# Constant scalars read from columns, a four-step split, and tokens routed quarter by quarter with their slots fetched by indirect transfers

## The reference, cut to what matters

```python
xn = layernorm(x)
s  = attn0(xn)               # 16 heads of 8, softmax over all 512 tokens of the row, out projection
g  = silu(ffn0(xn))          # each token goes to the expert of its largest logit, 1 of 8:
                             # gelu(xn @ W1[e]) @ W2[e], 128 -> 512 -> 128
x  = x + s * g
xn = layernorm(x)
s  = attn1(xn)               # 16 heads in windows of 32, and 8 heads over 64 pooled latents, gated
g  = silu(ffn1(xn))          # two layers: shift, qkv, l2norm, rotary, local attention, gated feed-forward
out = x + s * g
```

## Time and profile before

| | before |
|---|---|
| median of the runs | 3473.93 us (3471.63 to 3474.02, 3 runs) |
| the profiled execution | 3440.83 us, its span 3439.0 us, mean granted TensorE clock 0.974 |
| TensorE busy | 3112.3 us, 90% of the span |
| VectorE busy | 2466.9 us, 72% |
| ScalarE busy | 2338.7 us, 68% |
| GpSimd busy | 1261.4 us, 37% |

### The profile page before, as it was taken

The page is one execution under the profiler, slowest core; times in us unless marked ns, Lnnn a source line. Parts: engine busy times, 40 slices in busy tenths (PEclk is TensorE's granted clock), DMA queues, the critical chain, the costliest instruction groups (busy, mean ns, idle before and its releaser), DMA issues.

```text
span 3439.0 us, 83502 instructions
## 1 busy us (share of the span) xinstructions
PE 3112.3 (90%) x34007; PEld 1889.5 (55%) x34008; DVE 2466.9 (72%) x5000; ACT 2338.7 (68%) x4758; POOL 1261.4 (37%) x799
## 2 busy tenths in 40 slices
PE   5589799999999999999999999999999999999976
PEld 5168445556564646555565656565555656464644
DVE  6432487868687877878676868778786868687643
ACT  1265467777777786777767776867777777778744
POOL 1622034333333443444333333444443333344343
PEclk9889899999999999999999999999999999999987
DMA  6256110101011111101011111111010101111000
...
DMA packets 130458, 138.95 MB, mean 40 GB/s; under 512 B 17972, under 2 KB 112542, under 8 KB 129566
## 3 DMA queue, kind: packets, MB, share of 16 engines
...
## 4 chain that ended last, share of the span: by engine, by line
PE 46%; DVE 21%; ACT 9%; POOL 6%; issue 4%; DMA 2%; SPq 2%; POOLq 0%; ACTq 0%; DVEq 0%
PE bank L1882 5%; PE bank L1319 4%; DVE turn_f L2056 4%; PE bank L698 4%; PE bank L1926 3%; ACT prob_a L1388 3%; PE bank L1303 3%; PE bank L1332 3%; DVE nmax_a L1443 3%; PE bank L1868 3%; PE bank L1858 2%; PE bank L1849 2%; DVE ss L2049 2%; DVE nmax_f L2063 2%; POOL turn_f L1797 2%
## 5 line engine op out<-in xcount | busy, mean ns | idle before, releaser
L1388 ACT ACTIVATE prob_a<-bank 128x512 f32<-128x512 f32 x1024 | 564.4, 607 | 190.0 <-PE bank L1332 185.2
L1443 DVE TENSOR_REDUCE nmax_a<-bank 128x1 f32<-128x512 f32 x768 | 502.5, 684 | 161.6 <-PE bank L1303 160.5
L1791 POOL TENSOR_TENSOR rn<-ss,minus_half 128x16 f32<-128x16 f32 x128 | 377.8, 2952 | 270.6 <-DVE ss L2051 268.6
L1814 POOL TENSOR_TENSOR rs_f<-rs_f,minus_half 128x4 f32<-128x4 f32 x32 | 32.6, 1018 | 1108.2 <-DVE rs_f L1181 1108.2
L1797 POOL TENSOR_TENSOR turn_f<-turn_f 128x512 f32<-128x512 f32 x256 | 324.3, 1287 | 207.7 <-DVE turn_f L2056 207.7
L1332 PE MATMUL bank<-Qst_a,Kst_a 74*128 74x512 bf16 x1024 | 378.9, 389 | 18.9 <-ACT prob_a L1388 9.5
L1944 ACT ACTIVATE area<-bank 128x512 f32<-128x512 f32 x640 | 349.9, 603 | 63.2 <-PE bank L1882 55.2
L2056 DVE TENSOR_TENSOR turn_f<-area,rotf 128x1024 f32<-128x1024 f32 x256 | 307.6, 1219 | 8.7 <-POOL area L1801 6.2
L1303 PE MATMUL bank<-Kst_a,Qst_a 72*128 72x512 bf16 x768 | 302.2, 394 | 5.4 <-DMA Kst_a<-dk_a 1.2
L1319 PE MATMUL bank<-prob_a,V_a 128*9 128x512 f32 x2048 | 274.5, 609 | 13.2 <-ACT prob_a L1388 11.8
L1801 POOL TENSOR_TENSOR area<-turn_f,rn 128x1024 f32<-128x1024 f32 x128 | 267.5, 2090 | 19.0 <-POOL turn_f L1797 0.9
...
## 6 DMA issues: line engine op xcount, KB each, us to landing
...
```

The lines of the kernel that those rows point to most:

```text
L1388: nc.scalar.activation(dst, bk.full(act, product)[0:rows, :], func, **kw).then_inc(a_emptied["act"], 1)
L1443: nc.vector.tensor_reduce(out=nmax_a[:, g, t, j:j + 1], in_=bk.full(dve, f)[:], op=ALU.max, axis=AX.X, negate=True).then_inc(emptied, 1)
L1791: nc.gpsimd.tensor_tensor(rn[:, t % 2], ss[:, t % 2], minus_half[:], ALU.pow).then_inc(f_root, 1)
```

## The change

In the steady rows:
- `split` has four steps: the last subtraction writes the third bf16 part itself.
- The two copies of `split_max` become multiplications by a column of ones, `one_c`; the constants 1.0 of the gates and 1e-24 of the clip are read from columns too (`one_c`, `tiny_c`).
- The 0.5 of both gates is multiplied once into weights (`wo0_s`, `bo0`, `w_out_s`), and the last instruction of each gate becomes a plain addition.
- The 1/8 of the pooling goes into the two steps that follow it (`blocks_l` and the copies to `V_l`).

In the opening:
- VectorE chooses experts by quarters of 16 tiles (`choose`, eight instructions of 128 columns; a key of 8 minus the expert's number replaces the seven steps). TensorE ranks a quarter by expert and then by token with 23 matmuls (`ranks`), which makes each token's row within its quarter; three instructions (`rows_of`) bring it out.
- `xs_d` has 8192 rows, sorted within each quarter. GpSimd scatters a quarter's tiles from then on (`sort`), split around the last inverse root and the first weight loads. There is no zero fill.
- After the last quarter VectorE works out counts and bases, then a table of the row of `xs_d` for each of 39 x 256 slots (`m_slots`), then `pos`.
- Slots are fetched by GpSimd with two indirect gathers per block (`slots`) and no longer by SP. It issues them up to four blocks ahead, after the transposes of the block that had the ring's place (`m_slotT`).
- The first quarter is normalised right after its statistics, and GpSimd takes the first three inverse roots ahead of the head's. The early small loads are ten where they were seven; new are three tables (`expert_key`, `quarter_row`, `slot_at`).

All tables of order (`OPEN`, `TIMES`, `SEATS`) are new, and `STEP` is 179.028 where it was 177.917. In the new order 71 of row 0's 153 attention elements stand ahead of the first block's transposes, and the other 82 between the transposes and matmuls of the first blocks, the bulk ahead of block 13.

```diff
+        one_c, tiny_c = sb("one_c", [P, 1]), sb("tiny_c", [P, 1])
+        blocks_l = sb("blocks_l", [NL, LH])
...
-        xs_d = nc.dram_tensor("xs_d", [SLOTS, E], F32, kind="Internal").ap()
+        xs_d = nc.dram_tensor("xs_d", [B * T, E], F32, kind="Internal").ap()
...
             yield 5
             sp.wait_ge(s_zeroed, 1)
-            zeros, rows = turn_f[:].rearrange("p r t -> p (r t)"), xs_d.rearrange("(p r) f -> p (r f)", p=P)
-            fills = range(0, SLOTS * E // P, 4 * T)
-            for at in fills:
-                n = min(4 * T, SLOTS * E // P - at)
-                sp.dma_start(rows[:, at:at + n], zeros[:, 0:n]).then_inc(m_filled, 16)
...
-                if j + XS < NBLK:
-                    sp.dma_start(slot_ring[:, (j + XS) % XS], slot_rows(xs_d, j + XS)).then_inc(m_xs[j % XS], 16)
...
+            def inverse_root(c):
                 pool.wait_ge(m_var, c + 1)
                 nc.gpsimd.tensor_tensor(m_rs[:, c % 2, 1, :], m_rs[:, c % 2, 0, :], m_half[:], ALU.pow).then_inc(m_rstd, 1)
+
+            def sort(tiles):
+                for n in tiles:
+                    nc.gpsimd.indirect_dma_start(
+                        out=xs_d, out_offset=bass.IndirectOffsetOnAxis(ap=m_row[:, n:n + 1], axis=0),
+                        in_=x_tile(n), in_offset=None).then_inc(m_sorted, 16)
+
             def weights(j):
                 nc.gpsimd.indirect_dma_start(
                     out=w_ring[j % WS], out_offset=None, in_=W12,
                     in_offset=bass.IndirectOffsetOnAxis(ap=m_offs[:, j:j + 1], axis=0)).then_inc(m_w[j % WS], 16)
 
-            yield 82
-            pool.wait_ge(m_filled, 16 * len(range(0, SLOTS * E // P, 4 * T)))
-            pool.wait_ge(m_pos, 2)
-            for j in range(WS_EARLY):
-                weights(j)
-            for n in range(TILES):
-                nc.gpsimd.indirect_dma_start(
-                    out=xs_d, out_offset=bass.IndirectOffsetOnAxis(ap=pos[:, n:n + 1], axis=0),
-                    in_=x_tile(n), in_offset=None).then_inc(m_sorted, 16)
-            for j in range(WS_EARLY, NBLK):
-                yield block_slot(j - WS_EARLY) - 3
-                if j == WS_EARLY:
+            def slots(j):
+                for c in range(ST):
+                    nc.gpsimd.indirect_dma_start(
+                        out=slot_ring[:, j % XS, c], out_offset=None, in_=xs_d,
+                        in_offset=bass.IndirectOffsetOnAxis(ap=m_slots[:, j, c:c + 1], axis=0)).then_inc(m_xs[j % XS], 16)
+
+            for c in range(3):
+                yield 15 + 7 * c
+                inverse_root(c)
+            yield 38
+            pool.wait_ge(m_pos, 1)
+            sort(range(0, 6))
+            yield 46
+            inverse_root(3)
+            sort(range(6, 16))
+            for c in range(1, 4):
+                yield 50 + 12 * c
+                pool.wait_ge(m_pos, c + 1)
+                sort(range(16 * c, 16 * c + 8))
+                if c == 3:
+                    yield 91
+                    pool.wait_ge(m_pos, 5)
+                    for j in range(WS_EARLY):
+                        weights(j)
+                yield 56 + 12 * c
+                sort(range(16 * c + 8, 16 * c + 16))
+            for j in range(NBLK):
+                yield block_slot(j - XS) - 1
+                if j == 0:
+                    pool.wait_ge(m_pos, 6)
                     pool.wait_ge(m_sorted, 16 * TILES)
-                if j >= WS:
-                    pool.wait_ge(m_y, j - WS + 1)
-                weights(j)
+                if j >= XS:
+                    pool.wait_ge(m_slotT, j - XS + 1)
+                slots(j)
+                if j >= WS_EARLY:
+                    yield block_slot(j - XS) + 1
+                    if j >= WS:
+                        pool.wait_ge(m_y, j - WS + 1)
+                    weights(j)
             yield block_slot(NBLK) + 9
...
+            def ranks(c):
+
+                pe.wait_ge(m_hot, c + 1)
+                ps, first = rank_bank(c), 16 * c
+                nc.tensor.matmul(ps, tri[:], hot_bf[:, first:first + 16, :], start=True, stop=False, skip_group_check=True)
+                for m in range(15):
+                    last = nc.tensor.matmul(ps[:, NX * (m + 1):].rearrange("p (n e) -> p n e", e=NX), ones_sq[:],
+                                            hot_bf[:, first + m:first + m + 1, :].to_broadcast([P, 15 - m, NX]),
+                                            start=False, stop=False, skip_group_check=True)
+                for e in range(NX - 1):
+                    last = nc.tensor.matmul(ps.rearrange("p (n e) -> p n e", e=NX)[:, :, e + 1:], ones_sq[:],
+                                            m_held[:, c, e:e + 1].unsqueeze(1).to_broadcast([P, 16, NX - 1 - e]),
+                                            start=False, stop=(e == NX - 2), skip_group_check=True)
+                last.then_inc(m_ranks, 1)
...
+                if r % 4 == 1 and r > 4:
+                    yield 22 + 2.5 * r
+                    ranks(r // 4 - 1)
             row_logits(B - 1)
             yield 67.5
-            pe.wait_ge(m_hot, 1)
+            ranks(3)
...
+            def choose(c):
+
+                dve.wait_ge(m_logits, 4 * c + 4)
+                n = slice(16 * c, 16 * c + 16)
+                bias, key = (row.unsqueeze(1).to_broadcast(tiles_e) for row in (bg_s[:], expert_key))
+                top = m_max[:, n].unsqueeze(2).to_broadcast(tiles_e)
+                link(nc.vector.tensor_tensor(logit[:, n], by_expert(logit_bank(c)), bias, ALU.add))
+                link(nc.vector.tensor_reduce(out=m_max[:, n], in_=logit[:, n], op=ALU.max, axis=AX.X))
+                link(nc.vector.tensor_tensor(first_e[:, n], logit[:, n], top, ALU.is_equal))
+                link(nc.vector.tensor_tensor(first_e[:, n], first_e[:, n], key, ALU.mult))
+                link(nc.vector.tensor_reduce(out=m_max[:, n], in_=first_e[:, n], op=ALU.max, axis=AX.X))
+                link(nc.vector.tensor_tensor(hot_bf[:, n], first_e[:, n], top, ALU.is_equal))
+                link(nc.vector.tensor_reduce(out=m_sum[:, c, :], in_=hot_bf[:, n].rearrange("p n e -> p e n"), op=ALU.add, axis=AX.X))
+                nc.vector.tensor_copy(m_held[:, c, :], m_sum[:, c, :]).then_inc(m_hot, 1)
+
+            def rows_of(c):
+
+                dve.wait_ge(m_ranks, c + 1)
+                n = slice(16 * c, 16 * c + 16)
+                link(nc.vector.scalar_tensor_tensor(out=place[:, n], in0=by_expert(rank_bank(c)), scalar=float(c * (B * T // 4)),
+                                                    in1=hot_bf[:, n], op0=ALU.add, op1=ALU.mult))
+                link(nc.vector.tensor_reduce(out=m_posf[:, n], in_=place[:, n], op=ALU.add, axis=AX.X))
+                nc.vector.tensor_copy(m_row[:, n], m_posf[:, n]).then_inc(m_pos, 1)
...
+            for half in (bo0, wo0_s):
+                last = nc.vector.tensor_scalar(half[:], half[:], 0.5, None, ALU.mult)
+            link(last)
...
+            for at, step, c in ((14, normalise, 0), (18, statistics, 1), (22, normalise, 1), (26, statistics, 2), (30, choose, 0),
+                                (33, normalise, 2), (37, rows_of, 0), (38, statistics, 3), (43, choose, 1), (46, normalise, 3),
+                                (49, rows_of, 1), (53, choose, 2), (58, rows_of, 2), (62, choose, 3), (66, rows_of, 3)):
+                yield at
+                step(c)
...
-            while step < TILES:
-                nc.vector.tensor_copy(scan[1 - now][:, 0:step], scan[now][:, 0:step])
-                link(nc.vector.tensor_tensor(scan[1 - now][:, step:], scan[now][:, step:], scan[now][:, 0:TILES - step], ALU.add))
-                step, now = 2 * step, 1 - now
...
+            for q in (0, 4):
+                link(nc.vector.tensor_tensor(weighed, m_cmp.unsqueeze(1).to_broadcast([P, 4, NBLK, NX]),
+                                             m_step[:, q:q + 4, :].unsqueeze(2).to_broadcast([P, 4, NBLK, NX]), ALU.mult))
+                link(nc.vector.tensor_reduce(out=m_picked[:, q:q + 4, :], in_=weighed, op=ALU.add, axis=AX.X))
...
+                    nc.vector.tensor_scalar(blocks_l[:], blocks[0:NL, 0:LH], 1.0 / POOL, None, ALU.mult)
+                    nc.vector.tensor_scalar(w_out_s[:], w_out_s[:], 0.5, None, ALU.mult)
...
             link(nc.vector.tensor_copy(parts[1], res))
             yield at + 0.3
-            link(nc.vector.tensor_tensor(res, res, parts[1], ALU.subtract))
-            yield at + 0.4
-            nc.vector.tensor_copy(parts[2], res).then_inc(inc, 1)
+            nc.vector.tensor_tensor(parts[2], res, parts[1], ALU.subtract).then_inc(inc, 1)
 
         def split_max(link, nmax, mhi, parts, inc):
 
-            link(nc.vector.tensor_copy(mhi, nmax))
-            nc.vector.tensor_copy(parts[0], mhi)
+            link(nc.vector.tensor_scalar(mhi, nmax, one_c[:, 0:1], None, ALU.mult))
+            nc.vector.tensor_scalar(parts[0], mhi, one_c[:, 0:1], None, ALU.mult)
```

(19 more changed lines are left out.)

216 lines of the change are left out of this document (114 added, 102 removed), and 440 rows, old and new, of tables (OPEN, TIMES).

## The result

| | before | after |
|---|---|---|
| median of the runs | 3473.97 us (3471.63 to 3482.16, 4 runs) | 3596.84 us (3588.52 to 3603.53, 4 runs) |
| ratio, 95% interval | | 1.0348, 1.0317 to 1.038 |
| profiled execution | 3440.83 us, span 3439.0 | 3591.53 us, span 3589.7 |
| mean granted clock | 0.974 | 0.949 |

The change makes the kernel 3.5% slower. The forecast was 3439, in 3402 to 3472, with a chance of 0.11 for slower: the time is 158 us above the forecast and outside the range.

A forecast was written before the change was run, and what follows sets the result against it. The prediction took TensorE as the bound on average, with VectorE as second pole. Gains of 20 us (opening) and 15 (steady stages) sum to 35: profiled 3440.8 becomes 3406, the median 3473.9 becomes 3439, range 3402 to 3472.

The forecast's parts named there:

- the steady stages: Repeated row stages after the opening: 53 to 70 us less VectorE time, taken as 1 us a stage, 15 in all.
- Rival 4: Steady stages: the new order is worse by 3 us a stage, 45 over 15, giving 3484; chance 0.05.
- The column form is not held: Steady rows: GpSimd would not hold column instructions, saving VectorE 23.5 us (maxima's casts), 10.2 (clip) and 10.2 (first gate instruction).
- rival 3: Steady stages: column form held just the same, or TensorE takes no gain from shorter VectorE; 3451, chance 0.15.
- The split and the folds: Steady rows: VectorE loses the split's last cast (10.4 us) and the pooled sums' scaling (15.9); folded 0.5 removes no instruction.
- my 15: Steady stages: the total gain taken, 1 us a stage, between 0 and 50.
- The opening: Start of the kernel through the blocks: first block at 168 instead of 185.3, blocks 3 us shorter; gain 20 us.
- Logits with ranks: Opening: 44.2 us of logits plus 8.4 for three rounds of ranks and 9 of waits, done at 83.
- the routing: Opening, after the logits: some 26 us until TensorE resumes attention at 109, 15 later than before.
- The blocks: End of the opening: 182 us before, taken as 3 us less, ending at 347.
- rival 1: Blocks: GpSimd's slot transfers become the bound; 3493 at 6 us a block, 3529 at 6.9; chance 0.06.
- The 33 us between the profiled run and the median: Whole kernel: the median 3473.9 lay some 33 us above the profiled 3440.8, so 3406 profiled became 3439.

The follow-up runs named there:

- after_third: The changed kernel, unaltered, timed again in another job: 3541.96 us, ratio 1.0285.
- new_opening: The kernel before with only the new opening (routing by quarters, slots gathered by GpSimd, its order tables): 3441.82 us, ratio 1.0012.
- control_before: The kernel before, unaltered, run once more for its trace: 3437.02 us.
- folds_unpaced: The kernel before with the new opening, four-step split and folded 0.5 and 1/8; plain constants, old steady order, no waits between scatters: 3405.61 us, ratio 0.9896.
- paced: The changed kernel with GpSimd waiting before every eighth scatter until earlier ones have landed, run twice: 3548.22 us (1.0314) and 3547.06 us (1.0325).

## Why the prediction was wrong

**The step that failed** is the last sentence of the steady stages: "The order was re-planned everywhere; that moves instructions, adds none, and I cost it at 0, with up to 3 us a stage either way." It cost 8.8 a stage alone (197.5 against 188.6; 125 us in the time) and is the main cause of the result. The hint was even in the shown material: I had seen a cast held by L1801 on the chain, and the mean of 566 ns beside 175 said that it was one of many, and I treated their length as a property of the instruction. It is a property of where the order puts them against GpSimd's 1.9 and 2.5 us of work, and a new order draws these lengths anew. Rival 4 named it "for a reason that no row shows" at 3 us; the rows showed the reason.

**The column form is not held**: wrong. It is held in the same places, as rival 3 had it, and costs 60 ns more when free. All 29 that start within L1920 in after are held (1.74 to 1.81 us). By the Trainium skill, "SBUF — State Buffer", section "Who interferes with whom", copies, casts and tensor_scalar instructions can contend with GpSimd (no exception for a column is made), an instruction with two inputs in SBUF contends with a GpSimd instruction that reads SBUF, and tensor_reduce on trn2 never does; the traces agree on all three (29 of 29 columns held, 29 subtractions held, 28 reductions at 0.17 us). What misled me was row 0's normalise: four column instructions unstretched within two GpSimd instructions of 5.77 us together. But these were inverse roots. In after 56 normalise instructions start within such a root (L1910) and take 338 to 347 ns; the clip once, 234; the gate once, 743, its free time. Only GpSimd's rotary sums (L1916) and scalings (L1920) were seen to hold. I had a witness for the instruction and not for the kind of work beside it. Its 60 ns stood in the prediction as an upper bound of 17 us; rival 3, with 3451 only 12 us above the forecast, left out that the lengthened chain meets the next GpSimd instruction (15 subtractions at 1.88 for 0.17 us, 26 us of VectorE) and can tip the gate's race (8 to 18 us, below). The run of columns alone cost 50 us (3484.84 against 3435.16).

**The split and the folds**: right in kind and over-sized. 26 us of VectorE's instructions went, and the old order's period fell by 0 to 0.6 us, 0 to 9 in 15 stages, nearer to rival 3's "the chain gets some 3 of them" than to my 15.

**The opening**: its result was right, partly by luck, since two wrong terms cancel. In after_third:

| | forecast | measured |
|---|---|---|
| first TensorE matmul | 21 to 22 | 21.02 |
| logits done | 83 | 76.3 |
| attention's scores again | 109 | 100.3 |
| first block | 168 | 158.3 |
| last block's last matmul | 347 | 347.8 |
| row 0's places | 351 | 351.5 |

Logits with ranks took 7 us less than my sum and the routing 2 less; one round of ranks is 1.6 us against my 2.8 in the initial run of after. The blocks took 189.5 us (158.3 to 347.8) instead of 179, more than before's 182, which gave that back. No wait on slots from GpSimd shows in the block windows (TensorE busy 161.2 of the last 166.2 us): costed at nothing, rightly, and rival 1 didn't come. In new_opening the gain at the first copy is there (349.9 against 371.5 in control_before) and not in the time (1.0012): the interval behind it is 110.1 us instead of 102.3, and the period 189.8 instead of 188.4, on the same rows' code. The windows over the 14 periods, of new_opening and of control_before, say of what kind the loss is:

```profile
460.00:3117.70 2657.70, 2510.38 (x28700) 1489.15 (x28700) 2077.91 (x4058) 1945.84 (x4048) 1007.75 (x603) 0.99 0.11 29
```

```profile
473.70:3111.90 2638.20, 2497.84 (x28708) 1479.90 (x28704) 2087.53 (x4063) 1947.33 (x4052) 1007.87 (x604) 1.00 0.11 30
```

VectorE is busy no longer. Of the 19.5 us, 12.5 are longer matmuls at the lower mean clock and 7.0 are idle time of TensorE. In folds_unpaced the gain at the first copy is in the time. Why the clock and the idle time differ, no run here tells.

**The 33 us between the profiled run and the median.** I added them to my forecast as if they belonged to any kernel. They belong to the job: the kernel before has 3430.6 to 3438.5 in four jobs, near its profile of 3440.8, and 3468.6 and 3474.0 in two, whose profiles of the changed routing have the stretches. For after, the profiled run is 5 below the median: profile and runs are of the same kind. The stretches cost after about 55 us at row 0's places (406.8 against 351.5); before, by its medians, loses about 33 in such a job (no trace shows them in before itself), so the ratio moves little: 1.0348 and 1.035 with them, 1.0285 without (paced 1.0314 and 1.0325). They are 7 to 18% of the result, the order most of the rest.
